# A selective-scan block on one core: the skip matmul goes behind the second sum over states

## The reference

```python
u_inner = u @ W_in.T + b_in
x, z = split(u_inner, 2)                   # 512 channels each
delta = softplus(delta_raw @ W_dt.T + b_dt) # delta_raw, B, C come out of x @ W_x.T + b_x
def step(h, xs):                            # over the 2048 tokens; h is 512 x 16
    h = h * exp(dt_t * A) + x_t * dt_t * Bt
    y_t = einsum('bdn,bn->bd', h, Ct)       # sum over the 16 states
y = y + x * D                               # the skip
y = y * (z * sigmoid(z))
return y @ W_out.T + b_out
```

## Time and profile before

| | us |
|---|---|
| median of three executions | 2069.94 |
| the profiled execution's own time | 2073.05 |
| its span | 2071.2 |
| DVE busy | 1829.5 (88%) |
| POOL busy | 1805.5 (87%) |
| PE busy | 1750.8 (85%) |
| ACT busy | 1427.0 (69%) |

### The profile page before, as it was taken

How to read it: one execution, slowest core, us unless ns; L and a number is a source line. 1 busy time by engine, 2 the same in 40 slices (tenths; PEclk the granted TensorE clock), 3 DMA queues, 4 the chain that set the end, 5 groups by cost and what they waited for, 6 DMA issues and landing times.

```text
span 2071.2 us, 27781 instructions
## 1 busy us (share of the span) xinstructions
PE 1750.8 (85%) x7776; PEld 957.2 (46%) x7776; DVE 1829.5 (88%) x2230; ACT 1427.0 (69%) x2755; POOL 1805.5 (87%) x796
## 2 busy tenths in 40 slices
PE   3355679898988989888898989889898989898998
PEld 1112245444545545444554545454454545444475
DVE  2799999999999999989999999999999999999810
ACT  3566777777677777767777776777677677866522
POOL 1999999998989899998999989898999989899601
PEclk8686889999999999999999999999999999998999
DMA  5645464445536544553654455365544535554000
GB/s 174 146 108 121 116 148 119 108 115 125 130 84 151 119 119 114 123 134 72 150 119 113 111 131 133 74 150 119 130 112 114 142 81 123 118 146 112 13 8 13
DMA packets 146768, 235.04 MB, mean 113 GB/s; under 512 B 22064, under 2 KB 46896, under 8 KB 146096
## 3 DMA queue, kind: packets, MB, share of 16 engines
q1 hardware_dynamic: 146608, 233.18, 46.4%
HBM read 190.11 MB, written 42.99 MB: 113 GB/s over the span
## 4 chain that ended last, share of the span: by engine, by line
PE 51%; DVE 15%; POOL 13%; issue 11%; DMA 4%; ACT 3%; SPq 1%; DVEq 0%; POOLq 0%; ACTq 0%
PE bank L644 12%; PE bank L593 8%; POOL hs L1066 7%; PE y_ps L659 6%; PE bank L639 6%; PE bank L626 5%; DVE decay L986 5%; PE bank L607 5%; DVE hs L976 4%; POOL hs L1078 4%; DVE hs L986 3%; PE bank L597 2%; DMA dx_rep<-rep_scratch 2%; PE bank L587 2%; POOL z_dt L1023 2%
## 5 line engine op out<-in xcount | busy, mean ns | idle before, releaser
L1066 POOL TENSOR_TENSOR hs<-dx_rep,b_rep 128x2048 f32<-128x2048 f32 x256 | 1162.6, 4542 | 113.0 <-PE y_ps L659 100.0
L986 DVE TENSOR_TENSOR_SCAN decay<-decay,state,hs 128x512 f32<-128x512 f32 x640 | 796.5, 1276 | 47.5 <-ACT decay L798 42.1
L798 ACT ACTIVATE decay<-dt_rep,a_sb 128x512 f32<-128x512 f32 x1024 | 690.4, 685 | 26.8 <-DMA dt_rep<-rep_scratch 8.5
L986 DVE TENSOR_TENSOR_SCAN hs<-decay,state,hs 128x512 f32<-128x512 f32 x384 | 487.4, 1269 | 12.1 <-ACT decay L798 11.2
L1078 POOL TENSOR_TENSOR hs<-hs,c_rep 128x1024 f32<-128x1024 f32 x192 | 454.0, 2364 | 0.8 <-ACT state L812 0.7
L976 DVE TENSOR_TENSOR hs<-decay,c_rep 128x1024 f32<-128x1024 f32 x320 | 384.7, 1202 | 0.0
L659 PE MATMUL y_ps<-hs,nsum 128*32 128x512 f32 x2048 | 293.3, 652 | 87.3 <-POOL hs L1078 87.3
L644 PE MATMUL bank<-w_o_sb,r_t 128*128 128x256 f32 x1024 | 287.5, 443 | 64.9 <-DVE silu L883 63.3
L644 PEld LDWEIGHTS bank<-w_o_sb,r_t 128*128 128x128 f32 x1024 | 226.0, 225 | 119.8 <-DVE silu L883 72.7
L593 PE MATMUL bank<-xn_t,w_in_sb 128*128 128x512 f32 x512 | 247.1, 622 | 13.0 <-DVE silu L883 6.5
L639 PE MATMUL bank<-ident,r 128*128 128x128 f32 x1920 | 245.0, 281 | 10.7 <-ACT low_t L763 10.3
(11 more groups left out here) (101 smaller groups left out, 1763.6 us busy)
## 6 DMA issues: line engine op xcount, KB each, us to landing
dx_rep<-rep_scratch SPq DMA_DIRECT2D x256, 256.0 KB, 4.7
dt_rep<-rep_scratch SPq DMA_DIRECT2D x256, 256.0 KB, 7.6
b_rep<-bc_scratch SPq DMA_DIRECT2D x256, 64.0 KB, 2.1
rep_scratch<-z_dt SPq DMA_DIRECT2D x64, 256.0 KB, 2.5
rep_scratch<-e_dt SPq DMA_DIRECT2D x64, 256.0 KB, 2.7
c_rep<-bc_scratch SPq DMA_DIRECT2D x256, 64.0 KB, 2.1
xin<-in_u SPq DMA_DIRECT2D x16, 512.0 KB, 4.4
xr<-in_u SPq DMA_DIRECT2D x16, 512.0 KB, 4.0
```

Source lines behind the costliest of these rows:

```text
L798: nc.scalar.activation(decay[:, j, :], dt_rep[m % 2][:, j, :], ACT.Exp, scale=a_sb[:, J * s + j:J * s + j + 1]).then_inc(decay_ready, 1)
L986: v.tensor_tensor_scan(hs[s % 4][:, j, :] if kept else decay[:, j, :], decay[:, j, :], hs[s % 4][:, j, :], state[:, b, n:n + 1], ALU.mult, ...
L1066: nc.gpsimd.tensor_tensor(hs[s % 4][:], dx_rep[m % 2][:], b_rep[:, k, :].unsqueeze(1).to_broadcast([P, J, T]), ALU.mult).then_inc(input_re ...
```

## The change

`sum_states` no longer begins a block with the skip matmul. The four matmuls of the first sum (k = 0) carry `start=True`, each for its quarter of the bank, and the skip matmul is issued behind the second sum (k = 1) and behind its `nsum_done`, with `start=False`. The wait for `gated_ready` stays where it is, ahead of the block's first matmul. No other engine's code changes, and the number of instructions stays.

```diff
                 if k == 0:
                     at_least(pe, gated_ready, M * c + m)
-                    pe.matmul(y_ps[:], skip[:, m, :], x_t[odd][:, m, :], start=True, stop=False, skip_group_check=True)
...
                 for j in range(J):
-                    mm = pe.matmul(y_ps[32 * j:32 * j + 32, :], nsum[:], hs[s % 4][:, j, :], start=False,
+                    mm = pe.matmul(y_ps[32 * j:32 * j + 32, :], nsum[:], hs[s % 4][:, j, :], start=k == 0,
                                    stop=k == KG - 1, skip_group_check=True)
                 mm.then_inc(nsum_done, 1)
+                if k == 1:
+                    pe.matmul(y_ps[:], skip[:, m, :], x_t[odd][:, m, :], start=False, stop=False, skip_group_check=True)
```

## The result

| | before | after |
|---|---|---|
| median of four executions each, us | 2069.74 (2068.56 to 2070.49) | 2100.06 (2098.76 to 2102.92) |
| the profiled execution's own time | 2073.05 | 2098.76 |
| its span | 2071.2 | 2096.9 |

The ratio is 1.0149 (95% interval 1.0131 to 1.0167), so the change costs 30.3 us. The forecast was +42.7 in a range of +10 to +60: right in sign and inside the range, with 12.4 us too many.

What follows compares the result with a forecast made beforehand. DVE's own work, plus places where PE answers too late, was taken to set the end. Terms 11.2 + 19.5 + 12.0 = 42.7 us on the median of 2069.94 gave 2112.6, say 2112, range 2080 to 2130.

Steps and rivals of the forecast that it cites:

- Block 0, exposure: Skip behind Y3, hidden in the wait for xin, becomes new work ahead of T2 and Y0: 13 x 0.86 = 11.2 us.
- The clock behind the new pause: Behind Y3's restart full clock returns 6.8 to 8.9 us on, not 4.8; PE loses 1.5 a chunk, 19.5 us.
- Rival 4: Faster: behind Y3 the skip costs 2.07 us at low clock, 0.86 after moving; Y0's wait vanishes; 2059, chance 0.06.
- rival 1: Skips exposed in blocks 0 and 3, clock as before, T2 10.8 us behind the restart; 23.2 us, 2093, chance 0.22.
- row at 1020.27: Where PE restarted at 1020.27 and worked all the time, the clock was still 0.50 after 5.73 us.
- chunks take 122 to 123 us: Sign that the forecast is right, over the whole chunk; a chunk of 119.5 us or less would speak against it.
- Block 1: Skip moves along an unbroken PE stretch, ahead of C0 in both orders, so C0 keeps its time: cost 0.
- Blocks 2 and 3: Skips moved ahead of J7 and K3 delay DVE side by side, together 0.86 us in 14 chunks: 12.0 us.
- rival 5: Slower: K2 falls wholly into low clock, another 1.3 us per chunk gives 17, so 2129; chance 0.07.
- 2: Rival: DVE has hidden room at Y0 or K3, so only one term of 12 stays: 2082; chance 0.12.
- 3: Rival: no change, all moved work falls into PE's waits, 12 us of 119.5 a chunk: 2070; chance 0.08.

Runs made afterwards that it cites:

- noskip: Kernel before with all four skip matmuls left out, the first sums opening the bank; 2110.57 us, ratio 1.0195.
- twice0: Kernel before with block 0's skip behind the second sum, plus a discarded copy in its old place; 2090.48 us, ratio 1.0098.
- late0: Kernel before with only block 0's skip matmul moved behind the second sum; 2099.70 us, ratio 1.0134.
- fillall: Kernel before with block 1's skip in the pause ahead of D0, plus zero-weight matmuls: three ahead of Y3's wait, four of K2, one of D0; 2017.81 us, 0.9752.
- late1: Kernel before with only block 1's skip matmul moved behind the second sum; 2070.17 us, ratio 0.9999.
- twice3: Kernel before with block 3's skip behind the sum of step 13, plus a discarded copy in its old place; 2084.64 us, ratio 1.0072.
- late2: Kernel before with only block 2's skip matmul moved behind the second sum; 2069.35 us, ratio 0.9994.
- fillafter: Changed kernel with matmuls filling pauses: five ahead of K2, two of D0, three of Y3, two behind the first sum, two ahead of sum 12; 2070.85 us, 1.0008.
- late3: Kernel before with only block 3's skip matmul moved behind the second sum; 2095.59 us, ratio 1.0123.

## Why the prediction was right, and where it was off

Averaged over the 13 restarts, T2 starts 10.28 us behind the restart in the kernel before, 11.35 in `noskip`, 11.36 in `twice0`, 12.14 in the changed kernel and 12.51 in `late0`. Single chunks differ by up to 1 us, so the next two paragraphs go by these averages.

**Block 0, exposure (0.86, 13 times): right, and slightly small.** The pause for xin, the unmoved A0 and the skip as new work ahead of T2 are all in the trace; `twice0` measures 1.08 us of delay at T2, and the trace of after 0.96 from the skip's start to T2's.

**The clock behind the new pause (1.5, 13 times): right in kind, too large in size.** It was asked to be back 6.8 to 8.9 us behind the restart, and is back after 6.6 to 8.4. At T2 the clock costs 1.07 us in `noskip`, where nothing else delays it; with the delay of `twice0` taken off for the exposure, it costs 0.8 in the changed kernel and 1.15 in `late0`. The forecast measured it against a clock that is back 4.8 us behind the restart. That holds for the chunk of the earlier trace rows and seven more. In five of the 13 T2 was already late in the kernel before (10.4 to 11.0 us), and in four of these the low clock already lasted 5.5 to 6.2 us, as the prediction's own row at 1020.27 shows; there less was left to lose. It also read the clock as low from the restart on; in that chunk it is at 1.00 until 1261.6, while the skip runs. Both terms together were 30.7 us, and T2's delay in after, 13 x 1.86, makes 24. `late0` measures 29.7, close to 30.7 but in part by luck, since its low stretch is longer and begins ahead of the restart.

Rival 4 falls with this, for there is no gain. By size alone rival 1 (skips exposed, clock as before, 2093) is nearer to the measured 2100 than the forecast (2112) is. What speaks against it is T2, at 11.6 to 12.6 us and not at 10.8, the length of the low stretch, and `noskip`. The sign "chunks take 122 to 123 us" came true in part: from Y3 to Y3 they take 121.8 on average, apart from the turn of the loop (119.9 before).

That the Trainium skill ("TensorE: Matmul & The Clock Gate", section "Part 1: The HAM clock gate") puts the ramp at under 1% of a typical span doesn't hold here: `noskip` loses 1.95% and `fillall` wins 2.48%, with VectorE as the busiest engine. The Trainium skill's section "HAM oscillation — how this bites in real kernels" on the same page agrees with the runs: a loop with a pause in every turn pays in every turn.

**Block 1 (0): right**, by `late1`.

**Blocks 2 and 3 (0.86, 14 times): near in size, by other parts.** At step 13 the wait rose by 1.1 us (the forecast had 0.86), the 0.54 behind it vanished as forecast, and K3's rose by 0.46 (0.86 in `twice3`): about 1.1 a chunk, some 14 us against 12.0.

**The step that was off is the sum.** It adds the parts that were moved and holds the rest of the chunk as it was; K2 it gave to rival 5 alone. The ledger by DVE's waits, averaged over the nine chunks that begin between 416 and 1396 us and carried to 13:

| term | forecast, us | measured, us |
|---|---|---|
| block 0, exposure and clock: scan behind T2, 2.15 a chunk (0.15 before) | 30.7 | 26 |
| the wait of 0.2 us for a decay 3 us behind Y3, in most chunks before, gone | 0 | -2 |
| blocks 2 and 3: steps 13 and 14, K3 | 12.0 | 14 |
| K2 in low clock: 1.1 to 1.5 us in 6 of 9 chunks, before in 2 | 0 | 8 |
| K1 and router's bank: 1.1 us in 8 of 9 chunks before, gone | 0 | -13 |
| sum | 42.7 | 33 (the rows of waits: 32.8) |

What is left down to the 25.7 of the profiled executions is the lower busy time. So the clock term of block 0 was some 5 us too large, and K1's gain of 13 us, partly offset by K2's 8, stood nowhere. This is the largest error. Before, DVE waits in eight of these nine chunks for K1 and then for the router's bank, in `late0` still in seven (0.4 to 0.8, and 0.3); in after in none. The trace shows that this is the clock: behind the same pause of 2.15 us ahead of D0, K1 runs at half clock for most of its length before (0.50 from 1190.0 to 1193.3) and at 1.00 throughout in after:

```profile
1187.99 0.51 PE L603 MATMUL bank<-dt_st,w_dt_st 128*128 128x512 f32 x1 [2.15 <-DVE dt_st L876]
1188.77 5.41 PE L644 MATMUL bank<-w_o_sb,r_t 128*128 128x256 f32 x16 [0.28 <-DVE silu L883]
1194.22 0.42 DVE L898 TENSOR_TENSOR x<-bank,x 128x256 f32<-128x256 f32 x1 [0.83 <-PE bank L644]
```

```profile
833.95 0.50 PE L603 MATMUL bank<-dt_st,w_dt_st 128*128 128x512 f32 x1 [2.15 <-DVE dt_st L877]
834.74 3.72 PE L644 MATMUL bank<-w_o_sb,r_t 128*128 128x256 f32 x16 [0.29 <-DVE silu L884]
```

The first three lines are of the kernel before, the last two of after. What kept the clock up there is open: no run isolates it. The likely reason, argued and not shown, is that with the restart's low clock ending later the later low stretches fall elsewhere too. Neither block 1 nor block 2 alone does it (`late1` keeps 27 waits for K and 11 for lg, `late2` 29 and 11). It is one part of why the effects don't add up: 29.7 + 25.6 alone, 30.3 together; the other is sum 12, told above.

**Rivals.** 1 and 4 are dealt with. 2 ("one of the two places only", 2082) and 3 (2070) fall by size, and both places show in the trace. (Against 2 the prediction says that PE is the last in three waits in a row; it is in two, and the decays wait for ACT.) 5 came true in its mechanism in six chunks of nine, and was more than paid for by K1.

**What stays open:** the price of the order alone with all pauses filled, since `fillafter` mixed it with ill-placed fillings; `twice0` and `twice3` bound it only by parts, each with a clock of its own, and what block 0 alone showed at full clock is 0.75 us at T2.

## What to carry to other kernels

A matmul that stands in a pause of PE is not merely free: here it also kept the clock up for what followed. Moving it out can cost twice, once as exposed work at its new place and once as half clock at the old one, and the effects of several such moves on the clock don't add, so time them together. Compare averages over all turns of a loop: in the kernel before, T2 starts 9.9 us behind the restart in one turn and 11.0 in another. Where PE has pauses in every turn of a loop, fill them with thrown-away matmuls before re-ordering anything, sized so that they end ahead of what they wait for; it won 2.5% here in a kernel that by busy time VectorE bounds.

## What the runs showed of the hardware

- Taking matmuls away made the kernel slower: 128 PE instructions fewer, +40.1 us (`noskip`).
- Matmuls with weights of zero hold the clock as others do: behind 3.70 us of them K2 took 3.72 us, where it took 5.41 behind a pause of 3.87.

```profile
1191.65 3.70 PE L677 MATMUL y_ps<-w_i_sb,zeros 128*128 128x512 f32 x8
1195.68 3.72 PE L645 MATMUL bank<-w_o_sb,r_t 128*128 128x256 f32 x16 [0.33 <-DVE silu L894]
```

- The length of one pause didn't decide. A pause of 1.8 us was followed by half clock (`late3`, ahead of sum 12), and one of 0.9 us too (`fillafter`), while 0.77 with a skip matmul ahead of it was not the earlier trace rows. The same pause of 2.15 us ahead of D0 was followed by half clock in the kernel before and by full clock in after.
